# Moving gate, modulation and statistics work within the last three units of an attention loop

## What is computed

```python
h = _layernorm(x, axis=-1) * (1 + ca) + sa
x = x + ga * _L0_attn_ref(h, ...)      # 32 heads, 8 samples, head size 128
h = _layernorm(x, axis=-1) * (1 + cb) + sb
x = x + gb * _L0_ffn_ref(h, ...)       # 4 experts of rank 16, best 2 kept
h = _layernorm(x, axis=-1) * (1 + ca) + sa     # second block's own factors
x = x + ga * _L1_attn_ref(h, ...)
```

## Time and profile before

| | us |
|---|---|
| median of 3 runs | 1922.8 |
| lowest, highest | 1921.92, 1923.2 |
| the profiled execution | 1924.54 |
| its span in the trace | 1922.8 |
| TensorE matmul busy in it | 1839.8 (96%) |
| VectorE busy | 1511.7 (79%) |
| ScalarE busy | 924.2 (48%) |
| POOL busy | 906.4 (47%) |

### The profile page before, as it was taken

The page is one execution under the profiler, slowest core; times in us unless marked ns, Lnnn a source line. Parts: engine busy times, 40 slices in busy tenths (PEclk is TensorE's granted clock), DMA queues, the critical chain, the costliest instruction groups (busy, mean ns, idle before and its releaser), DMA issues.

```text
span 1922.8 us, 38262 instructions
## 1 busy us (share of the span) xinstructions
PE 1839.8 (96%) x12792; PEld 1546.2 (80%) x12792; DVE 1511.7 (79%) x2397; ACT 924.2 (48%) x2309; POOL 906.4 (47%) x872
## 2 busy tenths in 40 slices
PE   8999979999999999999999999997999988998997
PEld 5789968888888888888888888886888956666786
DVE  4677657888888888888888888887789658889887
ACT  3233324444444444444444444454655457888433
POOL 0133354444444444444444444364486557888111
PEclk9999989999999999999999999998999989999999
DMA  9677841111111111111111111221377776554121
GB/s 361 198 242 240 260 123 50 50 42 44 47 50 49 49 49 49 49 41 42 48 49 49 49 49 47 91 86 53 110 233 230 219 224 205 168 164 123 39 66 61
DMA packets 202712, 211.40 MB, mean 110 GB/s; under 512 B 19178, under 2 KB 172778, under 8 KB 201868
## 3 DMA queue, kind: packets, MB, share of 16 engines
q1 hardware_dynamic: 201124, 208.49, 35.2%
q10 hardware_dynamic: 1512, 1.90, 0.3%
HBM read 128.40 MB, written 73.53 MB: 105 GB/s over the span
## 4 chain that ended last, share of the span: by engine, by line
PE 66%; issue 13%; DVE 11%; POOL 4%; SPq 3%; DMA 2%; ACT 1%; DVEq 0%; POOLq 0%; ACTq 0%
PE ps L1125 18%; PE ps L1086 17%; PE ps L1099 7%; PE ps L1114 5%; PE ps L1137 4%; DVE f_neg_max L2082 4%; PE ps L1109 3%; SPq L1397 2%; POOL k_rot L631 2%; PE ps L2662 2%; PE ps L2698 2%; PE ps L2256 1%; PE ps L1898 1%; PE ps L2235 1%; DVE f_inv_sum L2088 1%
## 5 line engine op out<-in xcount | busy, mean ns | idle before, releaser
L1125 PE MATMUL ps<-wo,ot 128*128 (+1 forms) x1536 | 383.4, 399 | 0.0
L1125 PEld LDWEIGHTS ps<-wo,ot 128*128 128x128 f32 x1536 | 282.6, 190 | 55.4
L880 ACT ACTIVATE prob<-ps,neg_max 128x128 f32<-128x128 f32 (+1 forms) x512 | 208.2, 420 | 132.8 <-DVE neg_max L961 110.1
L1086 PE MATMUL ps<-ht_hi,wq 128*128 (+1 forms) x1024 | 255.1, 391 | 5.0 <-DVE q_swap L954 5.0
L1040 POOL TENSOR_TENSOR q_rot<-q_rot,q_swap 128x512 f32<-128x512 f32 x128 | 164.7, 1288 | 179.4 <-DVE q_swap L954 174.8
L887 ACT ACTIVATE pt<-ps 128x512 fp32r<-128x512 f32 x192 | 107.9, 597 | 280.0 <-PE ps L1137 279.9
L1086 PEld LDWEIGHTS ps<-ht_hi,wq 128*128 128x128 f32 x1024 | 193.5, 189 | 45.7 <-issue 5.4
L1034 POOL TENSOR_TENSOR prob<-prob,inv_sum 128x512 f32<-128x512 f32 x64 | 66.6, 1041 | 290.2 <-DVE inv_sum L970 290.0
L936 DVE TENSOR_TENSOR ot<-ps,ot 128x512 fp32r<-128x512 f32 x128 | 88.3, 691 | 75.3 <-ACT ot L897 75.3
L1099 PE MATMUL ps<-pt,vv 128*128 128x512 f32 x576 | 143.7, 394 | 3.4 <-issue 2.9
L631 POOL TENSOR_TENSOR k_rot<-k_rot,k_swap 128x512 f32<-128x512 f32 x32 | 60.2, 1883 | 181.1 <-DVE k_swap L535 181.1
(11 more groups left out here) (257 smaller groups left out, 4138.8 us busy)
## 6 DMA issues: line engine op xcount, KB each, us to landing
stack_dram<-e_part SPq DMA_DIRECT2D x192, 128.0 KB, 2.4
v_dram<-v_part SPq DMA_DIRECT2D x32, 512.0 KB, 5.7
k_dram<-k_part SPq DMA_DIRECT2D x64, 256.0 KB, 2.5
kk<-k_dram SPq DMA_DIRECT2D x128, 128.0 KB, 2.1
vv<-v_dram SPq DMA_DIRECT2D x128, 128.0 KB, 2.1
f_q<-stack_dram SPq DMA_DIRECT2D x124, 104.0 KB
f_k<-stack_dram SPq DMA_DIRECT2D x124, 104.0 KB
wmod<-in_wmod SPq DMA_DIRECT2D x12, 1024.0 KB, 14.4
```

Of the source, the lines that this page charges most:

```text
L880: nc.scalar.activation(p[:, h], sc[:, h], ACT.Exp, bias=neg_max[:, t, h:h + 1], accum_out=row_sum[:, t, h:h + 1]).then_inc(p_exp, 1)
L1086: mm = nc.tensor.matmul(ps_q[j][:], w[:, at:at + HD0], r[:, bass.ds(b, 2), k], start=(n == 0), stop=(n == len(passes) - 1))
L1125: mm = nc.tensor.matmul(ps_y[j][:], o[:, j, h * P:(h + 1) * P], w[:, bass.ds(at + h * D, D)], start=(n == 0), stop=(n == len(passes) - 1))
```

## The change

Four moves and one new wait. VectorE gets a hook behind the normalisation (`vector_normed`), to which `add_delta(0)` and `statistics(1, 0)` of step 63 and `statistics(0, 2)` of step 64 go; the statistics of steps 60 and 62 stay where they were. On ScalarE, `modulate(0, 1)` of step 63 goes behind the exponentials, and `root(1, 0)` behind the high parts of `pt`. POOL waits for `mid_ready` ahead of `residual(2)`, and behind its memset. On TensorE, `lora_in(0)` of step 62 goes behind `outputs(60, 0)`, directly ahead of the wait for `m_out` that was there.

```diff
--- before.py
+++ after.py
@@ -1002,6 +1002,7 @@
             accumulate(v - 2, 0)
             ahead.vector_middle(dve, v)
             normalize(v - 1)
+            ahead.vector_normed(dve, v)
             if v + 1 < U:
                 rotate(v + 1, (v + 1) % 4)
             rest_of_transposed(v - 1)
@@ -1530,9 +1531,7 @@
             routed(act, 0)
         if v == U0 - 2:
             lora_in_out(act, 0)
-        if v == U0 - 1:
-            act.wait_ge(r_done, 1)
-            modulate(act, 0, 1)
+
     def scalar_middle(act, v):
 
         if v == U0 - 4:
@@ -1540,12 +1539,15 @@
         if v == U0 - 2:
             root(act, 0, 1)
         if v == U0 - 1:
-            root(act, 1, 0)
+            act.wait_ge(r_done, 1)
+            modulate(act, 0, 1)
         if v == U0:
             modulate(act, 1, 0)
 
     def scalar_later(act, v):
 
+        if v == U0 - 1:
+            root(act, 1, 0)
         if v == U0:
             root(act, 0, 2)
             nc.scalar.preload_act_table(ACT.Exp)
@@ -1695,6 +1697,9 @@
             statistics(dve, 0, 0)
         if v == U0 - 2:
             statistics(dve, 0, 1)
+
+    def vector_normed(dve, v):
+
         if v == U0 - 1:
             add_delta(dve, 0)
             statistics(dve, 1, 0)
@@ -1790,6 +1795,7 @@
         if v == U0 - 3:
             pool.wait_ge(keep.first_q_done, queried(v))
             nc.gpsimd.memset(b0[:], 0.0).then_inc(b0_zero, 1)
+            pool.wait_ge(mid_ready, 1)
             residual(pool, 2)
         if v == U0 - 2:
             residual(pool, 3)
@@ -1850,9 +1856,6 @@
         if v == U0 - 3:
             pe.wait_ge(w_in, 48)
             router(pe, 0)
-        if v == U0 - 2:
-            pe.wait_ge(keep.first_q_mul, 2 * v + 2)
-            lora_in(pe, 0)
         if v == U0 - 1:
             pe.wait_ge(x2_step, 1)
             transposes(pe, 0, 1)
@@ -1861,6 +1864,8 @@
         if v == U0 - 3:
             pe.wait_ge(r_out, 2)
         if v == U0 - 2:
+            pe.wait_ge(keep.first_q_mul, 2 * v + 2)
+            lora_in(pe, 0)
             pe.wait_ge(m_out, 1)
         if v == U0 - 1:
             pe.wait_ge(modulated, 2 * KT)
@@ -1947,7 +1952,7 @@
     programs.scalar_start, programs.scalar_middle, programs.scalar_end = scalar_start, scalar_middle, scalar_end
     programs.vector_start, programs.vector_middle, programs.vector_later, programs.vector_end = (
         vector_start, vector_middle, vector_later, vector_end)
-    programs.scalar_later, programs.vector_last = scalar_later, vector_last
+    programs.scalar_later, programs.vector_last, programs.vector_normed = scalar_later, vector_last, vector_normed
     programs.gpsimd_end = gpsimd_end
     programs.tensor_middle, programs.tensor_free, programs.tensor_end = tensor_middle, tensor_free, tensor_end
     programs.sync, programs.scalar, programs.vector, programs.gpsimd, programs.tensor = sync, scalar, vector, gpsimd, tensor
```

## The result

Five runs each: the changed kernel's median is 1912.66 us (1912.45 to 1914.73), before 1922.71 us (1920.65 to 1923.2), ratio 0.9949 with a 95% interval of 0.9936 to 0.9962. By that ratio the change saves 9.8 us, between 7.3 and 12.3 (the two medians lie 10.05 us apart); 9.2 were forecast (1913.6 us), with a range of 1910.9 to 1917.0. The profiled execution took 1914.47 us around a span of 1912.7.

What follows compares the result with a forecast made beforehand. TensorE was taken to bound the kernel until it waits, with three waits in units 62 to 64. Gains of 5.2 + 3.1 + 0.9 = 9.2 us gave 1913.6 us, from a median of 1922.8; range 1910.9 to 1917.0.

Steps and rivals of the forecast that it cites:

- Part 1: Unit 62's gates and first residual add: with residual(2) behind mid_ready, gates take 2.37 us for 5.54, mid 3.1 us earlier.
- Part 2: Unit 62, lora_in behind outputs(60, 0): new pause 0.4 to 0.5 us, gain of the unit 5.2 us.
- The second rival: Unit 62's gates stay long, only accumulate and statistics come 2.1 us early; sum 6.1 us, 1916.7 us; chance 0.12.
- Part 3: Unit 63, modulate behind exponentials, add and statistics behind normalisation: normalisation 2.7 us earlier, gain 3.1 us, capped at 4.1.
- to move only one of the two would give 1.1 us or nothing: Unit 63: only ScalarE's modulate or only VectorE's add and statistics moved gives 1.1 us or nothing; both give 2.7.
- Part 4: Unit 64, statistics(0, 2) behind the normalisation: 0.9 us gained with a slow stretch, some 2.2 without; TensorE's wait 2.5 us.
- The clock: TensorE runs slow (1.2 GHz) after the new pauses of 2.1 and 2.5 us in units 63 and 64.
- the likeliest case: Units 62 to 64 gain 9.2 us, slow behind both later pauses: 1913.6 us, 1912.4 to 1914.8; chance 0.48.
- the first rival: Clock stays up in units 63 and 64, gains 4.1 and 2.2, sum 11.5 us: 1911.3 us; chance 0.30.
- the halves: Only one of the pauses in units 63 and 64 is harmless: 1912.4 us; counted within a rival's chance of 0.30.
- the third rival: The next stage takes the gain back, its SP queue meeting POOL's second halves late: 1921 to 1924 us; chance 0.06.
- the fourth: Four short pauses hold TensorE at 1.2 GHz from unit 62 to the end of 64: 1939 us; chance 0.04.

Runs made afterwards that it cites:

- e1: Kernel before with only POOL's wait for mid_ready ahead of residual(2); stage (near scores to the next stage's first head projection) 64.87 us for 71.28.
- e2: Kernel before with only lora_in(0) moved behind outputs(60, 0); stage 69.62 us for 71.28.
- e3: Kernel before with only VectorE's add_delta(0) and statistics(1, 0) of unit 63 moved behind the normalisation; stage 68.54 us for 71.28.
- e6: Kernel before with only statistics(0, 2) of unit 64 moved behind the normalisation; stage 68.40 us for 71.28.
- the repeat: The changed kernel run again without further edits; 0.9944 of the kernel before, stage 59.96 us for 60.19 the first time.
- e7: Changed kernel with the first reciprocal of units 63 and 64 ahead of the accumulation; stage 63.03 us for 60.19, total 0.9962 of the kernel before.
- e10: Changed kernel with lora_in(0) back ahead of outputs(60, 0); stage 60.65 us for 60.19, total 0.9954 of the kernel before.
- e8: Changed kernel with the first reciprocal ahead of the accumulation in unit 63 only; stage 59.27 us for 60.19, total 0.9930 of the kernel before.
- e9: Changed kernel, early first reciprocal in units 63 and 64, POOL's weight split waiting for p1's normalisation in 64; stage 57.33 us, 0.9937 of before.

## Why the prediction was right, and which of its steps were not

**Part 1** held at every number: 2.37 us for the gates (2.38), residual(2) ending 0.2 us before the normalisation (0.3 forecast), L1226 at 0.19. The lower bound of 0 is excluded by e1. What it did not say is how lopsided unit 62 is: I worked the gain of 5.2 us as that of two edits, and POOL's wait alone gives 5.1 of it, since TensorE's pause is shorter by it as well (1.66 us for 4.83) and the outputs behind it ran at a granted clock of 1.00, in 3.00 us for 4.97.

**Part 2** held: normalisation of unit 62 5.3 us earlier (14.75 less 9.41), the new pause 0.36 us, about 1 us of waiting for `pt` low (0.95). The second rival's sum, 2.1 us with slow gates, is what e2 measured.

**Part 3** held in its sum. p0 of unit 63 is 18.45 us behind that of 62, from 21.16: 2.7 as forecast. The cap of 4.1 us with a full clock was 4.2 (45.88 less 36.30, less 5.3). A slow stretch costs 1.1 of it (1.0 forecast). One step failed: "to move only one of the two would give 1.1 us or nothing". It took the end of all eight exponentials as the start of the whole normalisation. e3 shows that POOL's half depends on the first four only (p0 2.6 us earlier with VectorE's half alone). The forecast of the two together didn't hang on that step. No run shows the 0.3 us allowed for POOL's key sum by itself; in the changed kernel the key sum took 1.44 us (1326.04 to 1327.48), and L1682, which starts at 1327.08, 1.47 for the 1.22 of the add before.

**Part 4** is the same step again, and there it mis-sized a term: "it starts at 1352.35: 0.9 us". p0 came 1.5 us earlier, both in e6 and in the changed kernel (from the transpositions of `d_xn_first` to p0 7.00 us for 8.45), as POOL starts at the first reciprocal and VectorE's half, 2.10 us where both halves start together, takes 1.55 where POOL's starts 0.57 us ahead of it. VectorE's half itself started where it was forecast (e6: 53.42 us into the stage for 53.46). TensorE's pause became 1.99 us, not 2.5.

**The clock** was forecast as slow behind both pauses. In each of the two profiles of the changed kernel it was slow behind one. So the likeliest case was not the one seen, nor was the first rival; the halves I had put into that rival were, with their 1912.4 us. With both slow the stage would have been about 61.3 us (an estimate from the two profiles), 10.0 us shorter, and the forecast of 9.2 lies 0.8 us under that, most of it part 4. The 11.1 us seen are these 10.0 and 1.1 for the one pause that was harmless. So it is in part luck that the median came within 0.9 us of the forecast: a term too small, a pause that did no harm, and the scatter of the code behind. Over all the profiles six of eleven pauses of 2.0 to 2.1 us were followed by slow groups.

**Sum.** "I let all of it through" cannot be tested finer than the scatter of the code that follows. By the ratios the totals moved by 9.8 and 10.8 us, the stage by 11.1 and 11.3. Nothing speaks for the third rival: the part behind the stage took 552.6 us before, and 555.4 and 552.0 in the two profiles of the changed kernel. Nor for the fourth: 3.4 us of the stage were at a granted clock of 0.50 in each of these, 17.1 before. The normalisations came 5.3, 8.0 and 11.0 us earlier (9.9 in the repeat), where 5, 8 and 9 were set as the test.

## What to carry to other kernels

When a group of tiny VectorE operations takes microseconds, look at what POOL does at that very moment, and try holding POOL's long job back by one wait. Here it gave 5.1 us of unit 62's 5.3: 3.2 at the gates, and 2.0 because the outputs behind TensorE's shorter pause (1.66 us for 4.83) ran at a granted clock of 1.00. Edits on one chain don't add up: moving `lora_in` gave 2.1 us alone, and 0.2 beside that wait. Ask of each consumer which of a producer's several signals it really waits for, since a half that is ready early can start early. But before one engine is let off early, look at what it will start next: in e7 POOL's split of 4.51 us, which no wait held back, started 0.86 us before the L977 that everyone waits for, and L977 took 4.72 us for 1.22. The order that had kept them apart was an accident of timing.

## What the runs showed that was not expected

- Pauses of TensorE of 1.99 to 2.14 us in units 62 to 64: eleven in these profiles, six followed by groups at a granted clock of 0.50, five not, the same kernel showing both. What decides between the two no run here shows. All seventeen of 3.44 us or more were followed by slow groups; none of the six of 1.39 to 1.66 us was (unit 62 of e1 and e10, unit 63 of e7, e8 and e9, unit 64 of e9).
- The same program's span varied from 1906.9 to 1912.7 us between two profiles, with 38.6 and 48.5 us at a granted clock of 0.50: 5.8 us for 9.9 us of slow clock.
- VectorE's L973 (L977 in e7) took 4.72 us behind a 4.51 us POOL operation that started 0.86 us before it, for 1.22 us without; it ended 1.07 us after POOL's. Where it starts beside POOL's half of 1.04 us it takes 2.10.
